# A graph network on one core: 56 first-stage tiles in fours for 48 in pairs, and a 224-word pause for a 320-word one behind each gather

## The chip, the cores and the metric

One core of a Trainium2 chip runs the whole program. The metric is the device time of one execution in microseconds (us). The kernel before took a median of 1958.26 us over 3 runs (1946.44 to 1959.8).

## What is computed

The input is 3125 nodes with 128 features each and 53125 edges, sorted by destination, each with one of 8 relations. Cut to its core:

```python
h = relu(layernorm(x))
for W, root, bias in ((W1, root1, b1), (W2, root2, b2), (W3, root3, b3)):      # three relational layers
    out = h @ root + bias
    for r in range(8):
        msg = where(edge_type == r, (h @ W[r])[src], 0)
        out += segment_sum(msg, dst) / max(count of edges of relation r into dst, 1)
    h = relu(out)
x = x + h
h = relu(layernorm(x))
x = x + batchnorm(relu((h + segment_sum(h[src], dst)) @ W1' + b1') @ W2' + b2') + h  # the last layer
```

## The kernel before, in words

The 53125 edges are cut into 416 tiles of 128 edges. For each relational layer L (0, 1, 2) TensorE first multiplies the node features with all eight relation matrices; the products (25 blocks of 128 nodes, 512 KB each) are stored by the SP queue as a table in device memory, `h_table`. Then, for every tile, GpSimd (POOL) issues one indirect DMA, a gather, that fetches the 128 rows that the tile's edges name into one of 24 slots of `rows` (line 1260; line 1281 for the first 11 tiles of layers 1 and 2, with the same cost). VectorE builds a small matrix `sel` per tile (`select`, line 966) that holds the weight of each edge in the column of its destination, and TensorE multiplies rows by `sel` into a sum in PSUM (`sum_tile`, line 564). Tiles are counted through all layers as G = 416 L + t.

Behind each gather GpSimd clears private words that nobody reads: `rest_a_while` (line 1244), a memset of `PAUSE` = 320 words in each of 128 partitions. In two ways gathers are held back: gather G, if even, waits until TensorE has finished the tiles up to G - 11 (`AHEAD_OF_PE` = 12, semaphore `s_mm`), and at a layer's start gathers wait for the table.

The first `FORE` = 48 tiles of layer 0 go another way, since the table of layer 0 is late. Their raw, normalised input rows are gathered while TensorE still makes the table (line 1249, each gather followed by two one-word memsets `beat`, the second waiting for the first, line 1238). `fore_tile` (line 582) then multiplies them by `fore_sel`, which keeps relations apart (384 columns, `fore_select`, line 915 on VectorE), into PSUM banks of 64 nodes. ScalarE copies each full bank (`key_whole`, line 744, two buffers), and `key_banks` (line 593) multiplies two banks at a time by the eight relation matrices into the sum of layer 0. VectorE's `match_tile` (line 944) counts edges for the weights of each tile; it needs a chunk of 16 tiles' keys, loaded by the SP queue (line 1107), and stays 8 tiles ahead of `select`.

How the two kinds of tile are mixed on TensorE is set by a list:

```python
head_order = [("fore", t) for t in range(FORE_RING)]                  # FORE_RING = 12
for t in range(FORE_RING, FORE, FORE_PACE):                           # FORE_PACE = 2
    head_order += [("tile", FORE + (t - FORE_RING) // FORE_PACE)] + [("fore", f) for f in range(t, t + FORE_PACE)]
HEAD = FORE + (FORE - FORE_RING) // FORE_PACE
```

VectorE follows it by batches: eight `select` (with eight matches), then the `fore_select` of the 8 * `FORE_PACE` first-stage tiles that stand beside them. `fore_select` f waits until TensorE has done first-stage tile f - 12, and TensorE waits at the first ordinary tile of each eight until all eight `select` are done.

Layer 1 also builds the dense adjacency that the last layer uses; layers 1 and 2 begin with `late_sums` (line 619, after tile 12). After layer 2 the last layer has no gathers and ends the program.

Of the kernel before, what the change touches and what calls it, by code (L numbers as in the profile page):

```python
# [2 lines left out]

# [13 lines left out]
P = 128  # L17
# [16 lines left out]
SLOTS = 24  # L34
BATCH = 8
FREE = 2
PAUSE = 320
AHEAD_OF_PE = 12
SELS = 32
CHUNK = 16  # L40
# [19 lines left out]
FILLS = 4  # L60
REGS = 16

FORE = 48
FORE_RING = 12
FORE_PACE = 2
FORE_SPAN = 48
FORE_LEAD = 18
KEY_BANK = 64
# [23 lines left out]
def gnn_kernel(nc, x, src_t, dst_t, type_t, limits, w_rel, root_w, bias_w,  # L92
# [17 lines left out]
    FORE_STEP = start_of[BATCH] - start_of[0]  # L110
    fore_start = [FORE_STEP * (t // BATCH) + STEP * (t % BATCH) - FORE_LEAD for t in range(FORE)]
    FORE_SLACK = max(P * t // DEG - FORE_LEAD - s for t, s in enumerate(fore_start))
# [60 lines left out]

    assert FORE % BATCH == 0

# [49 lines left out]
    with ExitStack() as ctx:  # L225
        def sb(name, shape, dt=F32):
            return ctx.enter_context(nc.sbuf_tensor(name, shape, dt))

        def sem(name):
            return ctx.enter_context(nc.semaphore(name))  # L230
# [32 lines left out]
        count = sb("count", [P, 2, BATCH])  # L263
        col_i = sb("col_i", [P, 1], I32)
        rest = sb("rest", [P, 4 * P])
        beat = sb("beat", [P, 1])
        slow = sb("slow", [P, 2, PAUSE])


# [141 lines left out]
        s_xn = sem("s_xn")  # L411
        s_xturn = sem("s_xturn")
        s_xT = sem("s_xT")
        s_beat = sem("s_beat")
        s_rested = sem("s_rested")
        s_row = [sem(f"s_row{n}") for n in range(SLOTS)]
        s_sel = sem("s_sel")
# [800 lines left out]
        def _(pool):  # L1218
# [10 lines left out]
            pool.wait_ge(s_src, 32)  # L1229
            pool.wait_ge(s_x0, 16 * GROUPS)  # L1230

            beats = itertools.count()

            def pause():
                made = next(beats)
                if made:
                    pool.wait_ge(s_beat, made)
                nc.gpsimd.memset(beat[:], 0.0).then_inc(s_beat, 1)

            def rest_a_while(G):  # L1240

                if G % 2 == 0 and G > FORE:
                    pool.wait_ge(s_rested, (G - FORE) // 2)
                done = nc.gpsimd.memset(slow[:, G % 2, :], 0.0)  # L1244
                if G % 2 == 1:
                    done.then_inc(s_rested, 1)

            for t in range(FORE):
                pool.indirect_dma_start(fore_rows[:, t, :], None, x0_table,  # L1249
                                        bass.IndirectOffsetOnAxis(ap=src_i[:, t:t + 1], axis=0)  # L1250
                                        ).then_inc(s_fore_row[t // BATCH], 16)
                pause()
                pause()
            pool.wait_ge(s_idx, 1)
            pool.wait_ge(s_flag, 1)
            fast = pool.value_load(flag[0:1, 0:1], min_val=0, max_val=1)
# [6 lines left out]
            with pool.If(fast != 0):  # L1263
                for L in range(GIN):
# [6 lines left out]
                    for t in range(0 if L else FORE, TILES):  # L1271
                        G = TILES * L + t
# [552 lines left out]
```

## Time and profile before

| | |
|---|---|
| median of 3 runs | 1958.26 us (1946.44 to 1959.8) |
| profiled execution: time, and span of its instructions | 1950.05 us, 1948.0 us |
| mean granted TensorE clock | 0.63 |
| busy: PE, DVE, ACT, POOL | 67%, 46%, 34%, 85% |

The profile comes from one execution. Engines are PE (TensorE; PEld its weight loads), DVE (VectorE), ACT (ScalarE) and POOL (GpSimd). A granted clock of 1.00 is 2.4 GHz and 0.50 is 1.2 GHz; between them is a mean over a stretch at both. The square brackets of a timeline row say how long the engine sat idle before the row and what ended it; "issue" means that it waited for nothing that the profile shows.

### The profile page before, as it was taken

What the parts mean: (1) busy time and instruction counts of PE and PEld (TensorE: products, weight loads), DVE (VectorE), ACT (ScalarE), POOL (GpSimd) and SP (SyncE); (2) the same over time, 40 slices, a digit from 0 to 9 for tenths busy, and PEclk for the clock granted to TensorE, in tenths of its full rate; (3) what the DMA queues carried; (4) which work ended last, traced back from release to release, by engine and by line L of the source; (5) the groups of instructions that cost most, each with busy time, mean ns of one, the idle gap of its engine ahead of it and who ended that gap; (6) DMA issues with size and microseconds to landing.
All of it is one profiled execution on the core that took longest, in us unless ns stands there. A gap on an engine that the chain in (4) does not pass through costs nothing.

```text
span 1948.0 us, 18786 instructions
## 1 busy us (share of the span) xinstructions
PE 1314.2 (67%) x4604; PEld 853.1 (44%) x4627; DVE 899.4 (46%) x3270; ACT 654.3 (34%) x1147; POOL 1663.3 (85%) x2550
## 2 busy tenths in 40 slices
PE   6798674747566786666676767676566565657677
PEld 2275343434344464343343434455444444444454
DVE  5485845444543266666566766651222212122213
ACT  5312200000000277777677776742001111102123
POOL 5768888888888888888888888888888888888882
PEclk9697755555555655657565756565567676757678
DMA  7552332323332311212121222231111111111111
GB/s 241 176 152 85 100 99 78 99 78 89 89 89 65 98 44 44 88 44 87 45 87 45 76 55 73 58 99 44 45 44 43 45 44 43 45 44 44 45 45 47
DMA packets 70011, 144.26 MB, mean 74 GB/s; under 512 B 23487, under 2 KB 37048, under 8 KB 69896
## 3 DMA queue, kind: packets, MB, share of 16 engines
q0 software_dynamic: 39840, 81.67, 16.6%
q1 hardware_dynamic: 29624, 60.67, 8.9%
q8 instruction: 41, 0.67, 0.2%
q10 hardware_dynamic: 432, 0.64, 0.1%
q14 instruction: 74, 0.61, 0.1%
HBM read 100.23 MB, written 42.67 MB: 73 GB/s over the span
## 4 chain that ended last, share of the span: by engine, by line
POOL 75%; issue 11%; PE 10%; DMA 3%; ACT 1%; DVE 1%; another core or an unknown queue 0%; SPq 0%; POOLq 0%; DVEq 0%
POOL rows L1260 53%; POOL slow L1244 22%; PE ps_h L533 3%; DMA rows<-h_table,idx 2%; PE ps_a L582 1%; PE ps_agg L564 1%; PE ps_agg L619 1%; PE ps_agg L593 1%; POOL rows L1281 1%; PE ps_h L671 0%; PE ps_a L671 0%; ACT early L735 0%; DMA x_rows<-in_x 0%; PE ps_agg L542 0%; DMA h_table<-scratch 0%
## 5 line engine op out<-in xcount | busy, mean ns | idle before, releaser
L1260 POOL DMA_INDIRECT rows<-h_table,idx x1175 | 1121.5, 954 | 215.7 <-issue 189.4
L564 PE MATMUL ps_agg<-sel,rows 128*128 128x64 f32 (+14 forms) x2764 | 755.0, 386 | 579.5 <-DMA rows<-h_table,idx 566.9
L564 PEld LDWEIGHTS ps_agg<-sel,rows 128*128 128x128 f32 x2764 | 627.9, 287 | 915.0 <-DMA rows<-h_table,idx 718.3
L966 DVE TENSOR_SCALAR sel<-iota,early,norm 128x64 f32<-128x64 f32 x1178 | 419.6, 429 | 496.7 <-PE ps_agg L564 493.9
L1244 POOL MEMSET slow<- 128x320 f32 x1200 | 462.7, 386 | 0.6
L1062 DVE TENSOR_TENSOR early<-ps_a,early 128x300 f32 x416 | 198.3, 477 | 218.6 <-PE ps_a L651 181.3
L848 ACT ACTIVATE scratch<-scratch,ones 128x300 bf16<-128x300 f32 x416 | 223.7, 538 | 116.1 <-PE ps_a L651 90.9
L533 PE MATMUL ps_h<-w_all,xT 128*128 128x512 f32 x300 | 228.5, 873 | 17.9 <-issue 17.2
L854 ACT ACTIVATE scratch<-iota,code_lo 128x300 f32<-128x300 f32 x416 | 226.5, 545 | 12.5
L944 DVE TENSOR_SCALAR_CACHE_REDUCE agg_s<-scratch,key_f 128x256 bf16<-128x256 int16 x416 | 196.5, 479 | 18.8 <-DMA scratch<-key_rows 14.0
L651 PE MATMUL ps_a<-scratch 128*128 128x300 bf16 x416 | 174.3, 420 | 2.9 <-DVE early L1062 1.2
L1051 DVE TENSOR_SCALAR scratch<-iota,code_lo 128x128 bf16<-128x128 f32 x416 | 153.9, 371 | 0.0
L755 ACT COPY stage<-ps_h 128x512 f32<-128x512 f32 x80 | 46.7, 585 | 242.9 <-PE ps_h L533 212.5
L760 ACT ACTIVATE xT<-ps_agg,vecs 128x512 f32<-128x512 f32 (+2 forms) x16 | 9.5, 591 | 294.8 <-PE ps_agg L564 294.5
L651 PEld LDWEIGHTS ps_a<-scratch 128*128 128x128 bf16 x416 | 97.0, 233 | 6.4 <-issue 6.1
L533 PEld LDWEIGHTS ps_h<-w_all,xT 128*128 128x128 f32 x300 | 68.6, 266 | 58.1 <-issue 51.2
L820 ACT CAST stage<-early 128x3072 bf16<-128x3072 uint8 x13 | 35.7, 2750 | 171.5 <-PE ps_a L671 143.4
L755 DVE COPY stage<-ps_h 128x512 f32<-128x512 f32 x50 | 34.2, 684 | 119.5 <-PE ps_h L533 118.9
L1249 POOL DMA_INDIRECT early<-x_table,early x48 | 45.7, 952 | 23.0 <-DMA x_table<-early 16.4
L820 ACT CAST w_all<-early 128x3072 bf16<-128x3072 uint8 x12 | 32.9, 2751 | 78.6 <-PE ps_a L671 76.8
L767 ACT ACTIVATE hid<-ps_agg,vecs 128x512 f32<-128x512 f32 (+3 forms) x10 | 5.3, 526 | 150.4 <-PE ps_agg L564 141.4
L671 PE MATMUL ps_a<-w_all,scratch 128*128 128x512 bf16 x104 | 40.3, 504 | 0.3
(159 smaller groups left out, 781.0 us busy)
## 6 DMA issues: line engine op xcount, KB each, us to landing
h_table<-stage SPq DMA_DIRECT2D x65, 512.0 KB
rows<-h_table,idx POOLq DMA_INDIRECT x1175
scratch<-key_rows SPq DMA_DIRECT2D x26, 544.0 KB
h_table<-scratch SPq DMA_DIRECT2D x10, 512.0 KB
x_rows<-in_x SPq DMA_DIRECT2D x6, 256.0 KB, 6.3
w_all<-in_W SPq DMA_DIRECT2D x3, 512.0 KB, 6.6
x_table<-early SPq DMA_DIRECT2D x6, 256.0 KB, 2.3
out<-early SPq DMA_DIRECT2D x6, 256.0 KB
```

Of the source, the lines that this page charges most:

```text
L533: nc.tensor.matmul(half_bank(L, b, half)[:], xT[:, block_of(b)], w_all[:, L, 4 * half:4 * half + 4, :].rearrange("p r o -> p (r o)"), star ...
L564: mm = nc.tensor.matmul(sums_of(L, k)[:, at:at + width], mine, sel[edges, G % SELS, in_window:in_window + width], start=False, stop=(t == ...
L651: nc.tensor.matmul(ps_a[a % A_BANKS][:, 0:HOT], low[:, a % HOTS, :], hot[:, a % HOTS, :], start=True, stop=True).then_inc(s_step, 1)
L755: copy(stage_of(H)[:, 512 * half:512 * half + 512], half_bank(L, b, half)[:]).then_inc((s_evA, s_evD)[half], 1)
L848: nc.scalar.activation(hot[:, a % HOTS, :], apart[:, a % 2, :], ACT.Relu, bias=ones[:, 0:1], scale=-1.0).then_inc(s_hot, 1)
L854: nc.scalar.activation(apart[:, a % 2, :], iota[:, EARLY:EARLY + HOT], ACT.Abs, bias=code[:, a:a + 1]).then_inc(s_apart, 1)
L944: done = nc.vector.tensor_scalar(match[:, t % BATCH, :], chunks[:, c % 2, at:at + 2 * P], key_f[:, t:t + 1], 0.0, ALU.is_equal, ALU.add, a ...
L966: done = nc.vector.tensor_scalar(mine, here, dst, weight, ALU.is_equal, ALU.mult)
L1051: nc.vector.tensor_scalar(low[:, a % HOTS, :], iota[:, EARLY:EARLY + P], lo_f[:, a:a + 1], None, ALU.is_equal).then_inc(s_low, 1)
L1062: nc.vector.tensor_tensor(mine, ps_a[a % A_BANKS][:, 0:HOT].rearrange("p (b d) -> p b d", d=REACH), mine, ALU.add).then_inc(s_add, 1)
L1244: done = nc.gpsimd.memset(slow[:, G % 2, :], 0.0)
L1260: pool.indirect_dma_start(rows[:, slot, :], None, table, bass.IndirectOffsetOnAxis(ap=column, axis=0)).then_inc(landed, 16)
```

## The change

`FORE` goes from 48 to 56 and `FORE_PACE` from 2 to 4: 56 tiles are made by the first-stage way, and behind the first twelve, one ordinary tile stands before each four of them. Layer 0 gathers 8 tiles fewer from the table, 11 ordinary tiles instead of 18 are mixed in (`HEAD` 67 for 66), and there are 7 banks of 64 nodes instead of 6. `PAUSE` goes from 320 to 224, and the first-stage gathers are followed by the same pause instead of the two `beat` memsets.

```diff
-PAUSE = 320
+PAUSE = 224
...
-FORE = 48
+FORE = 56
 FORE_RING = 12
-FORE_PACE = 2
+FORE_PACE = 4
...
-            beats = itertools.count()
-
-            def pause():
-                made = next(beats)
-                if made:
-                    pool.wait_ge(s_beat, made)
-                nc.gpsimd.memset(beat[:], 0.0).then_inc(s_beat, 1)
-
             def rest_a_while(G):
 
-                if G % 2 == 0 and G > FORE:
-                    pool.wait_ge(s_rested, (G - FORE) // 2)
+                if G % 2 == 0 and G:
+                    pool.wait_ge(s_rested, G // 2)
                 done = nc.gpsimd.memset(slow[:, G % 2, :], 0.0)
                 if G % 2 == 1:
                     done.then_inc(s_rested, 1)
...
-                pause()
-                pause()
+                rest_a_while(t)
```

VectorE, from the first twelve `fore_select` (128x384) to the first `select` (`sel`), before; 128x256 is a match, in eights with their reciprocal:

```order
L915 TENSOR_SCALAR early<-iota,rest,norm 128x384 x12
L944 TENSOR_SCALAR agg_s,count<-scratch,key_f 128x256 x8
L952 RECIPROCAL norm<-count 128x8
L944 TENSOR_SCALAR agg_s,count<-scratch,key_f 128x256 x8
L952 RECIPROCAL norm<-count 128x8
L944 TENSOR_SCALAR agg_s,count<-scratch,key_f 128x256 x8
L952 RECIPROCAL norm<-count 128x8
L966 TENSOR_SCALAR sel<-iota,early,norm 128x64
```

The same place of the change:

```order
L912 TENSOR_SCALAR early<-iota,rest,norm 128x384 x12
L941 TENSOR_SCALAR agg_s,count<-scratch,key_f 128x256 x8
L949 RECIPROCAL norm<-count 128x8
L941 TENSOR_SCALAR agg_s,count<-scratch,key_f 128x256 x8
L949 RECIPROCAL norm<-count 128x8
L941 TENSOR_SCALAR agg_s,count<-scratch,key_f 128x256 x8
L949 RECIPROCAL norm<-count 128x8
L941 TENSOR_SCALAR agg_s,count<-scratch,key_f 128x256 x8
L949 RECIPROCAL norm<-count 128x8
L963 TENSOR_SCALAR sel<-iota,early,norm 128x64
```

Eight more matches stand ahead of the first `select`, so 64 tiles are matched there instead of 56, and the match behind the first `select` is of tile 64, the first of the fifth chunk, instead of tile 56.

VectorE at the end of the first batch of eight `select`, before:

```order
L944 TENSOR_SCALAR agg_s,count<-scratch,key_f 128x256
L952 RECIPROCAL norm<-count 128x8
L915 TENSOR_SCALAR early<-iota,rest,norm 128x384 x16
L966 TENSOR_SCALAR sel<-iota,early,norm 128x64
L944 TENSOR_SCALAR agg_s,count<-scratch,key_f 128x256
```

And of the change:

```order
L941 TENSOR_SCALAR agg_s,count<-scratch,key_f 128x256
L949 RECIPROCAL norm<-count 128x8
L912 TENSOR_SCALAR early<-iota,rest,norm 128x384 x32
L963 TENSOR_SCALAR sel<-iota,early,norm 128x64
L941 TENSOR_SCALAR agg_s,count<-scratch,key_f 128x256
```

32 `fore_select` instead of 16 follow each batch.

TensorE at the end of the first-stage tiles, before (`ps_a` are their banks, `ps_agg` the sum of the layer; 128x128 x8 is `key_banks`):

```order
L564 MATMUL ps_agg0<-sel,rows 128x51
L564 MATMUL ps_agg1<-sel,rows 128x13
L582 MATMUL ps_a2<-early 128x384 x2
L593 MATMUL ps_agg0<-hid,w_all 128x128 x8
L564 MATMUL ps_agg0<-sel,rows 128x44
L564 MATMUL ps_agg1<-sel,rows 128x20
```

And of the change:

```order
L579 MATMUL ps_a2<-early 128x112
L579 MATMUL ps_a0<-early 128x272
L579 MATMUL ps_a2<-early 128x56
L579 MATMUL ps_a0<-early 128x328
L579 MATMUL ps_a0<-early 128x384 x2
L590 MATMUL ps_agg0<-hid,w_all 128x128 x8
L590 MATMUL ps_agg0<-hid,w_all 128x64 x8
L561 MATMUL ps_agg0<-sel,rows 128x37
L561 MATMUL ps_agg1<-sel,rows 128x27
```

The last pair of banks now has a seventh bank behind it, with a `key_banks` of its own, and the next ordinary tile (tile 67) comes after both.

## Rows read from the trace of the kernel before

**Rows 1.** POOL by line: count | busy us, mean ns of one | idle before, who ended it

```profile
L1260 POOL DMA_INDIRECT rows<-h_table,idx x1175 | 1121.5, 954 | 215.7 <-issue 189.4 <-DMA h_table<-scratch 17.7 <-PE ps_agg L564 8.6
L1244 POOL MEMSET slow<- 128x320 f32 x1200 | 462.7, 386 | 0.6
...
L1238 POOL MEMSET beat<- 128x1 f32 x96 | 11.5, 120 | 4.7 <-POOL beat L1238 1.9
...
L1814 POOL MEMSET const-float32-1.0<- 128x1 f32 x1 | 0.1, 98 | 0.0
```

**Rows 2.** The waits: engine line waited for: us in total, times, longest

```profile
PE ps_agg L564 <- DMA rows<-h_table,idx: 566.9, 748, 2.9
```

**Rows 3.** Windows: length, PE, PEld, DVE, ACT, POOL busy (count), PEclk, DMA share, GB/s

```profile
108.00:158.00 50.00, 47.35 (x244) 38.51 (x244) 48.55 (x174) 3.51 (x6) 41.39 (x60) 1.00 0.34 99
158.00:663.00 505.00, 322.81 (x944) 216.52 (x944) 238.07 (x1039) 41.50 (x61) 449.01 (x674) 0.55 0.30 88
702.00:1288.00 586.00, 402.84 (x1408) 243.48 (x1406) 383.70 (x1204) 427.59 (x826) 521.68 (x780) 0.59 0.23 65
1327.00:1911.00 584.00, 370.31 (x1433) 253.30 (x1450) 126.61 (x465) 94.71 (x89) 519.66 (x779) 0.66 0.18 44
```

**Rows 4.** POOL in order of time: start us, us, instruction [idle before, who ended it]

```profile
40.78 0.94 POOL L1249 DMA_INDIRECT early<-x_table,early  x1
...
42.14 0.94 POOL L1249 DMA_INDIRECT early<-x_table,early  x1
...
223.33 0.95 POOL L1260 DMA_INDIRECT rows<-h_table,idx  x1 [0.17 <-issue]
224.28 0.38 POOL L1244 MEMSET slow<- 128x320 f32 x1
224.83 0.95 POOL L1260 DMA_INDIRECT rows<-h_table,idx  x1 [0.16 <-issue]
```

**Rows 5.** POOL in order of time, where it stood still, a slow gather, the last gather

```profile
108.36 0.94 POOL L1260 DMA_INDIRECT rows<-h_table,idx  x1 [17.69 <-DMA h_table<-scratch]
...
158.35 0.95 POOL L1260 DMA_INDIRECT rows<-h_table,idx  x1 [3.84 <-PE ps_agg L564]
...
700.62 0.95 POOL L1260 DMA_INDIRECT rows<-h_table,idx  x1 [1.12 <-PE ps_agg L564]
...
1411.83 1.40 POOL L1260 DMA_INDIRECT rows<-h_table,idx  x1 [0.16 <-issue]
...
1910.89 0.95 POOL L1260 DMA_INDIRECT rows<-h_table,idx  x1 [0.17 <-issue]
```

**Rows 6.** DVE in order of time, head of layer 0

```profile
101.97 0.48 DVE L944 TENSOR_SCALAR_CACHE_REDUCE agg_s<-scratch,key_f 128x256 bf16<-128x256 int16 x1 [9.76 <-DMA scratch<-key_rows]
...
105.54 0.31 DVE L966 TENSOR_SCALAR sel<-iota,early,norm 128x64 f32<-128x64 f32 x1
...
110.76 8.62 DVE L915 TENSOR_SCALAR early<-iota,rest,norm 128x384 f32<-128x384 f32 x16
```

**Rows 7.** SP queue in order of time: loads of key chunks (L1107) and weights (L1172)

```profile
96.72 0.42 SPq L1107 DMA_DIRECT2D scratch<-key_rows  x1
...
103.59 1.49 SPq L1172 DMA_DIRECT2D w_all<-in_W  x2
105.12 47.91 SPq L1107 DMA_DIRECT2D scratch<-key_rows  x4
```

**Rows 8.** PE in order of time, head of layer 0

```profile
113.74 0.41 PE L564 MATMUL ps_agg<-sel,rows 128*128 128x64 f32 x2 [1.87 <-DMA rows<-h_table,idx]
...
146.48 1.52 PE L582 MATMUL ps_a<-early 128*128 128x192 f32 x8
...
153.29 3.98 PE L593 MATMUL ps_agg<-hid,w_all 128*128 128x128 f32 x16 [0.68 <-ACT hid L744]
```

**Rows 9.** Windows behind the head: the clock across a thin stretch (166 to 170 us)

```profile
166.00:170.00 4.00, 0.88 (x5) 0.49 (x3) 3.81 (x18) 0.58 (x1) 3.67 (x6) 1.00 0.82 257
170.00:175.00 5.00, 4.43 (x12) 2.57 (x13) 3.47 (x14) 0.00 (x0) 4.43 (x7) 0.60 0.32 105
```

More of the change, by code:

```diff
@@ L1 @@
-import itertools
 from contextlib import ExitStack
@@ L265, in gnn_kernel @@
         rest = sb("rest", [P, 4 * P])
-        beat = sb("beat", [P, 1])
         slow = sb("slow", [P, 2, PAUSE])
@@ L413, in gnn_kernel @@
         s_xT = sem("s_xT")
-        s_beat = sem("s_beat")
         s_rested = sem("s_rested")
```

## The prediction

> **What bounds the kernel now.** I read the lines of POOL first, then the waits, then the windows by stage, then POOL in order of time. POOL is 85% busy in the whole span, and two kinds of work make that up: 1175 gathers of 954 ns and 1200 pauses of 386 ns [rows 1]. What it does not spend on them is mostly a gap of 0.16 to 0.17 us between a pause and the next gather, which the view calls "issue": 189.4 us in total [rows 1]. In order of time an ordinary period is gather 0.95, pause 0.38, gap 0.17: starts at 223.33 and 224.83, 1.50 us apart [rows 4]. From 158 to 1911 us this runs almost without a break: POOL waits for TensorE only 8.6 us in the whole run, of which 3.84 at 158.35 and 1.12 at 700.62 [rows 1, 5]. Everyone else waits for the gathers: TensorE's tile matmuls stood 566.9 us in 748 waits for gathered rows [rows 2]. Its busy share is 64% (322.81 of 505 us) in layer 0, 69% in layer 1 and 63% in layer 2, at a mean granted clock of 0.55 to 0.66 [rows 3]. So the time from 158.35 to the last gather at 1910.89 is 1170 periods of GpSimd, and what remains is a head of 158 us and an end of 1948.0 - 1910.89 = 37.1 us.
>
> In the head it is different. From 108 to 158 us DVE is busy 48.55 and PE 47.35 of 50 us [rows 3], and POOL, though it starts at 108.36 when the table has landed, stands still in the end because it may run only 12 tiles ahead of TensorE [rows 5].
>
> **The pause: 96 words fewer.** No 224-word memset is in the trace. A memset of one word takes 98 ns alone and 120 as `beat`, one of 320 words 386 [rows 1]. The slope is (386 - 98) / 319 = 0.90 or (386 - 120) / 319 = 0.83 ns a word, so 96 words are 80 to 87 ns; I take 84. The bounds: nothing, if the period has a floor that the pause only fills; and 0.3 * 386 = 116 ns, if the whole duration scales with the words. 1170 periods by 84 ns are 98 us off (0 to 136). All of it lies on the path as long as TensorE keeps up: the period becomes 1.42 us, and the 69% share of layer 1 becomes 0.69 * 1.50 / 1.42 = 73%. That such a pace is possible for gathers is shown by the first stage, which ran at 42.14 - 40.78 = 1.36 us [rows 4].
>
> **The first-stage gathers.** 56 by about 1.42 us instead of 48 by 1.36 end some 14 us later, near 105 us, still before the table's landing at 108.36 [rows 5]. They are hidden; their 0.5 MB more beside the table's stores may push the landing by a microsecond, which I put into the head.
>
> **The head.** Here the change costs. The place to watch is tile 78's gather, which started at 158.35 [rows 5]: the periods behind it are the same tiles in both kernels. The 8 gathers that leave layer 0 buy nothing if this one starts no earlier. Its condition is TensorE past tile 67, and that tile stands behind all first-stage work.
> - DVE starts matching tiles 48 to 55 at 101.97, when its chunk has landed, and reaches the first `select` at 105.54 [rows 6], 3.4 us later. In the change eight more matches come first, so it is there near 109. Behind the first `select` it now needs tile 64, of a chunk whose load was issued at 105.12, behind two 512 KB weight loads at 103.59 [rows 7]. The chunk before it took 5.3 us, from its issue at 96.72 to DVE's use at 101.97 [rows 6, 7]. This one has more ahead of it: I take 113 to 114 us for its arrival (109 to 117). Then seven more pairs of `select` and match at 0.63 us: the eighth `select` ends near 118.5.
> - TensorE does its first ordinary tile then, at about 118.5 and not at 113.74 [rows 8]. That is 5 us lost, and an idle stretch of some 7 us.
> - From there, 44 first-stage tiles instead of 36. Two of them take 1.52 us [rows 8], so 8 more are 6.1 us. Seven ordinary tiles fewer at 0.2 give back 1.4.
> - At the end ScalarE must copy the seventh bank, into a buffer that the `key_banks` ahead of it is still reading. So TensorE waits about 1.2 us (before, it waited 0.68 for the sixth [rows 8]), and then does a `key_banks` of half the width: between a half and the whole of 3.98 us, I take 2.3.
> - Clock: after the thin stretch at 166 to 170 us TensorE's granted clock was 0.60, while it had been 1.00 in the head [rows 9, 3]. An idle stretch of 7 us in the head may do the same. I take 2 us for it (0 to 10).
>
> Sum: 5 + 6.1 - 1.4 + 0.5 + 2.3 + 2 + 1 (the landing) = 15.5. Tile 78's gather starts near 174 instead of 158.35: 15 us lost (5 to 27). DVE's 32 `fore_select` in a row do not add to it: two of them take 8.62 / 8 = 1.1 us [rows 6] and TensorE's two 1.5, so the ring of twelve stays full.
>
> The rule of the Trainium skill on the clock (TensorE: Matmul & The Clock Gate, Part 1) says that idleness takes the array to half its rate and sustained activity gives it back. By that rule the first-stage tiles behind the gap would start at half rate; the trace agrees in direction with 0.60 behind the thin stretch.
>
> **Starts of layers 1 and 2.** At 700.62 the gather waited 1.12 for TensorE, which had `late_sums` to do [rows 5]. That point follows from the tables and not from the pause, so the 26 gathers from the last of layer 0 gain nothing there: 26 * 84 ns = 2.2 us lost. At layer 2's start the same point was reached without a wait but close to it; I take 1.2.
>
> **Sum.** -98 + 15 + 3.4 = -79.6 us. Against the profiled execution: 1950.05 - 79.6 = 1870.5 (span 1868.4). The median of the runs lies 8 us higher, so the same sum gives 1878.7 there. I predict 1873.
>
> **Rivals.**
> - *TensorE takes over.* At 1.2 GHz its work per tile is near the new period wherever transforms or dense products are mixed in. For: granted clock 0.55 in layer 0 with 64% busy [rows 3]. Against: POOL waited 8.6 us in all. If a fifth of the 98 us is not given, 1893.
> - *A floor eats half.* The gather's own work could go on under the pause, so that shortening the pause moves the wait into the gather or the gap. For: the gap of 0.17 is unexplained. Against: 1.36 in the first stage. Half of 98 gives 1873 + 49 = 1922. The Trainium skill speaks for it (Perfetto Trace Analysis, DMA Instruction — SWDGE): the profile shows no start of such a DMA and ends it when the last descriptor is written, while the processor still has to finish the instruction. By that rule there is hidden work behind the 0.95 us; the row of 1.36 says that it is no floor at 1.42.
> - *The floor eats all of it.* Then the 98 us are missing: 1873 + 98 = 1971, within 1% of before.
> - *Slower: close gathers disturb each other.* A gather took 1.40 instead of 0.95 us at 1411.83 [rows 5]; few do now. If closer spacing made one in four do so, the mean grows by 0.25 * 0.45 = 0.11 us, 1170 of them 131 us: 1873 + 131 = 2004. It decides from a mean growth of 0.07 us (80 / 1170) on. For: the first stage ran at 1.36 us for 48 gathers only, not for 1170. Against: its gathers took 0.94 us, no more than those of the longer period [rows 4].
>
> **How the numbers follow.** The forecast has 0.70, TensorE as bound 0.07, half a floor 0.08, a whole one 0.04, slower 0.11. A measurement of this kernel can tell about 1% from no change. Faster by over 1% is 0.70 + 0.07 + 0.08 = 0.85, within 1% 0.04, slower 0.11. The pause at 80 to 90 ns and the head at 5 to 27 us give 1852 to 1893 for the forecast itself; the range goes up to half a floor, 1925.
>
> **What would show it.** Right: pauses of about 300 ns, gathers of 0.95, a period near 1.41 to 1.42, the eighth `select` near 118 us, tile 78's gather near 174 us, POOL waiting for TensorE some 25 us or more in the head alone, an end of 37 us behind the last gather. Wrong: gathers above 1 us in the mean, a gap that grew from 0.17, rows landing late with TensorE's waits unchanged, or POOL waiting for TensorE all through layers 0 and 1.

## The result and the profile after

The changed kernel takes 1935.01 us (median of four runs, 1931.12 to 1939.61) beside 1959.03 us for the kernel before: 0.9891 of it, with a 95% interval of 0.9843 to 0.9939. The direction of the prediction was right, its size wrong: 80 us were forecast, 24 came. The profiled execution took 1936.56 us, its span is 1934.5 us.

The costliest groups of the page of the changed kernel, as in [rows 1] and [rows 2] (busy us and mean ns of one, then the idle time before them and what ended most of it):

```profile
L1248 POOL DMA_INDIRECT rows<-h_table,idx x1167 | 1117.7, 958 | 282.6 <-issue 184.0
L561 PE MATMUL ps_agg<-sel,rows 128*128 128x64 f32 (+14 forms) x2748 | 674.4, 365 | 316.4 <-DMA rows<-h_table,idx 277.5
L1233 POOL MEMSET slow<- 128x224 f32 x1248 | 380.0, 305 | 0.9
L648 PE MATMUL ps_a<-scratch 128*128 128x300 bf16 x416 | 161.2, 388 | 245.3 <-issue 151.3
L1059 DVE TENSOR_TENSOR early<-ps_a,early 128x300 f32 x416 | 196.1, 471 | 247.6 <-remote 132.6
```

The pause took 305 ns where [rows 1] had 386: 81 ns less, as forecast. A gather takes 958 ns (954 before), and the gap is still 184.0 / 1167 = 0.16 us. So the gather has no floor of its own at this distance, and close gathers do not slow each other. But TensorE waited for rows only 277.5 us and not 566.9 [rows 2], and two groups that hardly waited before now do: the adjacency products of layer 1 on TensorE (L648, idle 245.3 us; 2.9 before) and VectorE's add behind them.

GpSimd in order of time answers to [rows 4, 5]. An ordinary period, then the table's landing, tile 78, tile 440 (layer 1), tile 448, tile 828 and tile 1246, the last gather:

```profile
start us, us, engine line op out<-in xcount [idle before <-releaser]
...
111.06 0.95 POOL L1248 DMA_INDIRECT rows<-h_table,idx  x1 [8.63 <-DMA h_table<-scratch]
...
175.96 0.95 POOL L1248 DMA_INDIRECT rows<-h_table,idx  x1 [12.48 <-PE ps_agg L561]
...
300.77 0.95 POOL L1248 DMA_INDIRECT rows<-h_table,idx  x1 [0.17 <-issue]
301.73 0.30 POOL L1233 MEMSET slow<- 128x224 f32 x1
302.19 0.95 POOL L1248 DMA_INDIRECT rows<-h_table,idx  x1 [0.17 <-issue]
...
706.47 0.95 POOL L1248 DMA_INDIRECT rows<-h_table,idx  x1 [8.88 <-PE ps_agg L561]
...
717.86 0.95 POOL L1248 DMA_INDIRECT rows<-h_table,idx  x1 [0.17 <-issue]
...
1280.16 0.95 POOL L1248 DMA_INDIRECT rows<-h_table,idx  x1 [1.06 <-remote]
...
1892.63 0.95 POOL L1248 DMA_INDIRECT rows<-h_table,idx  x1 [0.16 <-issue]
```

The ordinary period is 302.19 - 300.77 = 1.42 us, as forecast. The same tiles in both traces show where the time went (starts of the gathers; the sum, 13.5 us less, is the difference of the two profiled spans, while the medians lie 24 us apart):

| stretch, tiles | before | after | difference | forecast |
|---|---|---|---|---|
| up to tile 78 | 158.35 | 175.96 | +17.6 | +15.5 |
| 78 to 414, layer 0 | 503.40 | 484.74 | -18.7 | -28.2 |
| 414 to 448, start of layer 1 | 51.20 | 57.16 | +6.0 | -0.7 |
| 448 to 828, layer 1 | 571.23 | 562.30 | -8.9 | -31.9 |
| 828 to 864, start of layer 2 | 52.79 | 60.96 | +8.2 | -1.8 |
| 864 to 1246, layer 2 | 573.92 | 551.51 | -22.4 | -32.1 |
| behind the last gather | 37.1 | 41.9 | +4.8 | 0 |

(Forecast: 84 ns for each period, less the 2.2 and 1.2 us of the two starts.) The head came as forecast; the layers gave far less, and layer 1 least.

The head's own rows, VectorE first. Tile 48's match, the first `select`, the match that waits for the next chunk, the eighth `select`:

```profile
start us, us, engine line op out<-in xcount [idle before <-releaser]
103.90 0.48 DVE L941 TENSOR_SCALAR_CACHE_REDUCE agg_s<-scratch,key_f 128x256 bf16<-128x256 int16 x1 [15.72 <-DMA scratch<-key_rows]
110.85 0.32 DVE L963 TENSOR_SCALAR sel<-iota,early,norm 128x64 f32<-128x64 f32 x1
115.11 0.48 DVE L941 TENSOR_SCALAR_CACHE_REDUCE agg_s<-scratch,key_f 128x256 bf16<-128x256 int16 x1 [3.94 <-DMA scratch<-key_rows]
...
119.25 0.31 DVE L963 TENSOR_SCALAR sel<-iota,early,norm 128x64 f32<-128x64 f32 x1
```

And TensorE at both ends of the first-stage work:

```profile
start us, us, engine line op out<-in xcount [idle before <-releaser]
119.61 0.43 PE L561 MATMUL ps_agg<-sel,rows 128*128 128x64 f32 x2 [4.48 <-DVE sel L963]
120.80 2.93 PE L579 MATMUL ps_a<-early 128*128 128x384 f32 x4 [0.75 <-issue]
...
166.60 3.89 PE L590 MATMUL ps_agg<-hid,w_all 128*128 128x128 f32 x16
171.22 3.67 PE L590 MATMUL ps_agg<-hid,w_all 128*128 128x64 f32 x16 [0.73 <-ACT hid L741]
```

### The profile page after: what moved, and what is told of

The parts are those of the page before. It is cut to its first block, busy times and chain, and to the rows that moved or that the text cites. A ratio compares the mean times of both kernels' runs of the same rounds, so it can differ in the third digit from the quotient of the medians.

```text
span 1934.5 us, 18805 instructions
## 1 busy us (share of the span) xinstructions
PE 1232.1 (64%) x4633; PEld 867.5 (45%) x4656; DVE 857.4 (44%) x3270; ACT 644.0 (33%) x1148; POOL 1574.5 (81%) x2502
## 4 chain that ended last, share of the span: by engine, by line
POOL 37%; PE 21%; issue 19%; another core or an unknown queue 11%; ACT 6%; DVE 4%; DMA 2%; DVEq 0%; SPq 0%; ACTq 0%; POOLq 0%
POOL rows L1248 28%; POOL slow L1233 9%; PE ps_h L530 5%; PE ps_a L648 5%; PE ps_agg L561 5%; ACT scratch L845 4%; PE ps_a L579 2%; DVE early L1059 2%; PE ps_agg L616 1%; DMA rows<-h_table,idx 1%; ACT scratch L851 1%; PE ps_agg L590 1%; PE ps_agg L539 1%; DVE sel L963 1%
## 5 line engine op out<-in xcount | busy, mean ns | idle before, releaser
L1248 POOL DMA_INDIRECT rows<-h_table,idx x1167 | 1117.7, 958 | 282.6 <-issue 184.0
L561 PE MATMUL ps_agg<-sel,rows 128*128 128x64 f32 (+14 forms) x2748 | 674.4, 365 | 316.4 <-DMA rows<-h_table,idx 277.5
L963 DVE TENSOR_SCALAR sel<-iota,early,norm 128x64 f32<-128x64 f32 x1170 | 374.4, 363 | 516.7 <-PE ps_agg L561 349.5
L1233 POOL MEMSET slow<- 128x224 f32 x1248 | 380.0, 305 | 0.9
L648 PE MATMUL ps_a<-scratch 128*128 128x300 bf16 x416 | 161.2, 388 | 245.3 <-issue 151.3
L1059 DVE TENSOR_TENSOR early<-ps_a,early 128x300 f32 x416 | 196.1, 471 | 247.6 <-remote 132.6
L530 PE MATMUL ps_h<-w_all,xT 128*128 128x512 f32 x300 | 219.0, 839 | 54.9 <-issue 30.2
L941 DVE TENSOR_SCALAR_CACHE_REDUCE agg_s<-scratch,key_f 128x256 bf16<-128x256 int16 x416 | 192.6, 471 | 24.4 <-DMA scratch<-key_rows 19.7
L648 PEld LDWEIGHTS ps_a<-scratch 128*128 128x128 bf16 x416 | 54.3, 131 | 290.4 <-issue 280.0
L1048 DVE TENSOR_SCALAR scratch<-iota,code_lo 128x128 bf16<-128x128 f32 x416 | 133.9, 322 | 0.0
L1238 POOL DMA_INDIRECT early<-x_table,early x56 | 53.6, 957 | 25.3 <-DMA x_table<-early 16.3
L579 PE MATMUL ps_a<-early 128*128 128x384 f32 (+39 forms) x186 | 44.7, 389 | 0.9 <-issue 0.7
```

Source lines behind the costliest of these rows:

```text
L530: nc.tensor.matmul(half_bank(L, b, half)[:], xT[:, block_of(b)], w_all[:, L, 4 * half:4 * half + 4, :].rearrange("p r o -> p (r o)"), star ...
L561: mm = nc.tensor.matmul(sums_of(L, k)[:, at:at + width], mine, sel[edges, G % SELS, in_window:in_window + width], start=False, stop=(t == ...
L579: mm = nc.tensor.matmul(ps_a[j % A_BANKS][:, at:at + width], fore_rows[:, t, :], fore_sel[:, t % FORE_RING, in_window:in_window + width], ...
L648: nc.tensor.matmul(ps_a[a % A_BANKS][:, 0:HOT], low[:, a % HOTS, :], hot[:, a % HOTS, :], start=True, stop=True).then_inc(s_step, 1)
L941: done = nc.vector.tensor_scalar(match[:, t % BATCH, :], chunks[:, c % 2, at:at + 2 * P], key_f[:, t:t + 1], 0.0, ALU.is_equal, ALU.add, a ...
L963: done = nc.vector.tensor_scalar(mine, here, dst, weight, ALU.is_equal, ALU.mult)
```

## Where layer 1 went: the ring between TensorE and VectorE

In layer 1 every tile also brings an adjacency product (`pairs`, L648) into one of three PSUM banks, and VectorE's `add` (L1059) empties it. Product a waits for add a - 3. Paired one to one in the trace, 20 of the 416 products of the kernel before began within 0.25 us of that add's end, and 327 in the changed one. The add came 0.65 us (median) behind the start of its product before, and 3.1 us after. That is odd, because the same product takes no longer than before (388 ns in the mean, 420 before). ScalarE's copies of the table's halves show the same thing in two rows each. Changed kernel, layer 1: TensorE's product of a first half, then ScalarE's copy of it.

```profile
start us, us, engine line op out<-in xcount [idle before <-releaser]
1008.09 1.91 PE L530 MATMUL ps_h<-w_all,xT 128*128 128x512 f32 x2
...
1013.68 0.59 ACT L752 COPY stage<-ps_h 128x512 f32<-128x512 f32 x1 [2.36 <-remote]
```

The product's record ends at 1008.09 + 1.91 = 1010.00, ScalarE stood idle for 2.36 us and yet started only at 1013.68. The trace also holds the updates of the semaphores. I took, for each matmul that updates one, the time from its modelled end to the next update. In layer 1 it is over 0.5 us for 10% of them in the kernel before (median 0.01 us) and for 67% in the changed one (median 1.17). This way of counting has a flaw: where the record of an update is missing, the next one stands in for it and looks late. In layer 1 of the kernel before 554 of TensorE's 622 updates are recorded, in the changed one 507 of 609. Counted the other way, from each recorded update back to the last modelled end, none is over 0.5 us late in the kernel before and 64% are in the changed one (median 1.0 us, the latest 7.3 us). The recorded updates of VectorE, ScalarE and GpSimd stand within 0.04 us of an end in both. So TensorE's completions, and only they, reach the others late. This is what the experiments had to explain.

## The experiments

**First occasion: the parts of the change, and the size of the pause.** Four kernels on one chip, kernel before 1951.93 us.

```diff
# e1, e3, e4: kernel before, only this line (224, 272, 128)
-PAUSE = 320
+PAUSE = 224
# e2: changed kernel
-PAUSE = 224
+PAUSE = 320
```

e1. 

> The kernel before with 224 instead of 320 words in each memset of the pause, and nothing else: 48 first-stage tiles, two between two others, the one-word beats as they were. In the changed kernel the median period fell as forecast (1.50 to 1.42 us), but tile 78's gather came 17.6 us later and layers 1 and 2 gave only some 9 and 22 us in place of 30. Theory A (the shorter period itself makes TensorE's completions late, so that the ring of three banks that its adjacency products share with VectorE's add paces layer 1): the same loss without any change in the first stage, so only the 17.6 us of the head come back: 1935 - 18 = 1917 us (1908 to 1926), and VectorE's add waits for TensorE all through layer 1. Theory B (the loss comes with the first stage's change, through an alignment of the tiles): the whole pause is given, 1959 - 98 + 3 = 1864 us (1855 to 1875).

e2. 

> The changed kernel with the pause put back to 320 words: 56 first-stage tiles, four between two others, and the memset pause in the first stage remain. Theory A: tile 78's gather is some 16 us late and nothing else is lost, TensorE's completions come on time again: 1959 + 15 = 1974 us (1968 to 1980). Theory B: the loss of some 40 us in layers 1 and 2 is here too, on top of the head: 2010 us or more.

e3. 

> The kernel before with a pause of 272 words, half of the step. 48 words are 1170 periods by 42 ns = 49 us. Theory A with a loss that sets in between (TensorE's late completions begin below some period): 1959 - 49 + 2 = 1912 us, as fast as the pause of 224 words or faster. Theory A with a loss in proportion (40 of 98 us): 1959 - 29 = 1930 us. Theory B: 1912 us, and slower than the pause of 224 words by 49 us.

e4. 

> The kernel before with a pause of 128 words: a period near 1.34 us if nothing else holds it. Theory A: no faster than with 224 words, 1900 to 1930 us, with GpSimd waiting for TensorE's count through all of layer 1 and in much of layers 0 and 2. Theory B, and no floor: 1959 - 1170 x 0.16 = 1772 us. If close gathers also disturb each other, gathers above 1 us in the mean and over 1935 us.

Measured:

| | us | ratio (interval) | us a tile in layers 0, 1, 2 | late updates in layers 0, 1, 2 |
|---|---|---|---|---|
| before, 320 words | 1951.93 | | 1.497, 1.503, 1.502 | 0%, 0%, 0% |
| e2, 320 words | 1957.15 | 1.0029 (1.0014 to 1.0044) | 1.497, 1.503, 1.501 | 0%, 0%, 0% |
| e3, 272 words | 1926.11 | 0.9863 (0.9827 to 0.9899) | 1.458, 1.483, 1.463 | 1%, 65%, 6% |
| e1, 224 words | 1911.81 | 0.9821 (0.978 to 0.9861) | 1.443, 1.478, 1.445 | 47%, 60%, 57% |
| e4, 128 words | 1922.84 | 0.9866 (0.9807 to 0.9925) | 1.448, 1.482, 1.445 | 62%, 56%, 64% |
| changed kernel | 1935.01 | 0.9891 (0.9843 to 0.9939) | 1.442, 1.480, 1.444 | 37%, 64%, 61% |

(Layer paces from the starts of the gathers of tiles 90 and 414, 448 and 828, 864 and 1246; "late" is the share of TensorE's recorded updates over 0.5 us behind the last modelled end. The paces and shares of before and of the changed kernel are those of their own profiles, and the changed kernel's time is from an occasion of its own.) Theory A holds and B falls: the loss is there with the pause alone (e1), and absent where only the first stage is changed (e2). e3 lies between its two figures for Theory A, nearer to the loss in proportion (1930 us). The loss depends on the distance of the gathers: with 320 words completions are prompt, with 272 they are late almost only in layer 1, with 224 everywhere, and below that the time gets no better. 1.44 us a tile in layers 0 and 2 and 1.48 in layer 1 is what TensorE then gives, whatever the pause. e2 cost 5 us and not 15, and its rows say why. The last store of the table, and TensorE's first ordinary tile:

```profile
start us, us, engine line op out<-in xcount [idle before <-releaser]
...
70.42 2.05 SPq L1084 DMA_DIRECT2D h_table<-scratch  x2
```
```profile
start us, us, engine line op out<-in xcount [idle before <-releaser]
...
110.36 0.66 PE L561 MATMUL ps_agg<-sel,rows 128*128 128x64 f32 x2 [29.34 <-DMA rows<-h_table,idx]
```

The last stores of the table were issued at 70.42, in the kernel before at 101.49 and in the changed one at 104.96. In the kernel before the gathers of the first stage stand 1.36 us apart [rows 4], here 1.50. e2 differs from the changed kernel in nothing but the words of the pause, which gave 1.42 us there. Between 20 and 100 us, while the table is made, 17 of the 43 recorded updates of TensorE are over 0.5 us late in the kernel before and none of 46 in e2. So the first stage's close gathers had held up the table in the kernel before too.

**Second occasion: the leash, the products, the kind of pause.** Another chip, kernel before 1935.28 us.

```diff
# e5: e1 and
-AHEAD_OF_PE = 12
+AHEAD_OF_PE = 20
# e6: e1 without lows(), hots(), pairs() and add() in layer 1
# e7: kernel before with
-PAUSE = 320
+PAUSE = 128
                 if G % 2 == 1:
                     done.then_inc(s_rested, 1)
+                pause()
# e8: e1 with
-FORE = 48
+FORE = 40
+FORE_PAUSE = 320
...
-                done = nc.gpsimd.memset(slow[:, G % 2, :], 0.0)
+                done = nc.gpsimd.memset(slow[:, G % 2, 0:FORE_PAUSE if G < FORE else PAUSE], 0.0)
...
-                pause()
-                pause()
+                rest_a_while(t)
```

e5. 

> The kernel of e1 (before with a pause of 224 words) with GpSimd allowed 20 tiles ahead of TensorE in place of 12. In e1 TensorE lags about ten us behind the gathers all through layer 1 and GpSimd touches its limit of 12 tiles again and again. If the limit is what costs (TensorE is late now and then, but fast enough on average), the longer leash gives back most of it: 1912 - 20 = 1892 us or less. If TensorE's own pace is the bound while the gathers are this close (my theory), the leash is only used up: 1905 to 1915 us, the same as e1, with a lag that grows to some 20 tiles' time.

e6. 

> The kernel of e1 with the adjacency products left out of layer 1 (no lows, no hots, no pairs, no add, so that the output lacks their part). In e1 layer 1 ran at (1251.39 - 689.89) / 380 = 1.478 us a tile, layers 0 and 2 near 1.445. If layer 1's loss is the ring of three banks between TensorE and VectorE, lengthened by TensorE's late completions, layer 1 falls to the pace of the other layers, 1.42 to 1.445: 380 x 0.035 = 13 us or more less, 1912 - 13 = 1899 us (1888 to 1902). If the completions are late for a reason that has nothing to do with what TensorE is doing, they are late here too and layer 1 gains nothing beyond that. If instead the close gathers have nothing to do with it and TensorE was simply full, layer 1 runs at 1.42 without any wait: 1890 us.

e7. 

> The kernel before with a pause of 128 words followed by a memset of one word that waits for the one before it, so that the period is put back to some 1.46 to 1.50 us with less than half of the words. If what makes TensorE late is the distance between the gathers (my theory), its completions are on time again outside layer 1 and GpSimd hardly waits: 1959 - 1170 x (1.50 - period), 1915 to 1959 us, above e4's 1923 where the period comes out at 1.47 or more. If it is the shortness of the memset itself (how long GpSimd's other units rest), they stay late as in e4 and the time is 1960 us or more.

e8. 

> The kernel of e1 with a pause of 320 words behind the first-stage gathers in place of two beats, and 40 of them in place of 48. In the run with 320 words everywhere the first stage's period was 1.50 us and the table's last stores were issued at 70.4 us, and at 101.5 in the kernel before, whose first stage ran at 1.36 us. If the close gathers of the first stage are what made the table late, the first table gather starts at 23 + 40 x 1.50 = 83 us without a wait for the table, and tile 78's near 140 us in place of 150.8: 1912 - 11 = 1901 us (1894 to 1905). If the early table of that run had another cause, GpSimd waits for it until 100 to 108 us again, with 8 tiles more to gather behind it: 1912 + 12 = 1924 us.

Measured: e5 1830.21 us (0.946, 0.9443 to 0.9477), e6 1837.48 (0.9496, 0.9479 to 0.9514), e7 1788.24 (0.9245, 0.9229 to 0.9261), e8 1838.71 (0.951, 0.9491 to 0.9528). All four came over 50 us below the figures expected for them. Not one update in these four traces came over 0.5 us late, neither in the head nor in the layers. The layers ran at 1.416 to 1.422 us a tile with 224 words and at 1.375 in e7 (e4's first two table gathers stand 107.72 - 106.39 = 1.33 us apart: the one-word memset adds only some 40 ns to that, so the period did not return to 1.46 us). These runs tell nothing on the leash or the ring; they say that the late completions may not be a property of the kernels alone, which the third occasion tests.

**Third occasion: is it the edits or where they ran?** Kernel before 1948.83 us. No kernel is new.

e9. 

> The changed kernel once more, unaltered. The last four kernels ran on another chip than the first four: there the kernel before took 1935 us and not 1952 to 1959, TensorE's semaphore updates came 0.01 us behind the modelled end of their matmul everywhere (on the first chip up to several us late wherever the gathers were 1.42 us apart), and a pause of 224 words gave 100 us and not 40. Theory C (how late TensorE's completions come behind close gathers depends on the chip, not on the kernel): where the kernel before is near 1935 us here, the changed one takes 1935 - 80 = 1855 us (1845 to 1865) by the prediction's own sum; where it is near 1955, 1935 us again. If the difference of the last runs came from their edits (a longer leash, no products, another first stage), the changed kernel is at 0.99 of the kernel before on any chip.

e10. 

> The kernel of e1 once more, unaltered: 224 words and nothing else. Theory C: 1935 - 98 + 3 = 1840 us (1835 to 1846) where the kernel before is near 1935 us, and 1912 us where it is near 1955. The difference to the changed kernel on the same chip is what the first stage's change costs: 15 us by the prediction, 23 on the first chip. If the edits made the difference and not the chip: 0.982 of the kernel before on any chip.

e11. 

> The kernel of e5 once more: 224 words and 20 tiles ahead in place of 12. Its first run has no twin with 12 on the same chip. Theory C: within 12 us of the kernel with 12 tiles where completions are on time (what GpSimd waited for in the head, 8 to 10 us, goes). Where they are late: the same as with 12 tiles if TensorE's mean pace is the bound, 20 us less or more if the limit is.

e12. 

> The kernel of e4 once more: 128 words. On the first chip it was no faster than 224 words (1923 to 1912 us). Theory C: where completions are on time there is no floor at 1.42 us, the period is 1.33, and the time 1840 - 1170 x 0.08 + 10 = 1756 us (1745 to 1775). With a floor of the gather's own between 1.33 and 1.42: 1790 us or more. On a chip like the first: 1920 us again.

Measured: e9 1929.15 us (0.9904, 0.987 to 0.9938), e10 1916.74 (0.9827, 0.9797 to 0.9856), e11 1921.63 (0.987, 0.9833 to 0.9906), e12 1917.67 (0.9834, 0.9799 to 0.987). All as on the first occasion, late completions included. The kernel of e5 took 0.946 of the kernel before there and 0.987 here: the edit is not the cause. e11 against e10 answers the question on the leash: with 20 tiles ahead TensorE's median lag behind a gather's start grew by 12 us in layer 1, from some 9 (changed kernel, and e10 within 0.3 us of it) to 21 us, layer 1 ran at 1.476 us a tile and not at 1.478, and nothing was gained. What holds is TensorE's pace while its completions are late, and not the limit on GpSimd. e9 - e10 = 12.4 us is the price of the first stage's change here.

**Fourth occasion.** Another chip, kernel before 1933.38 us. The kernels of e9, e6, e8 and e7.

e13. 

> The changed kernel, unaltered, for a chip of the kind on which e5 to e8 ran. There (the kernel before near 1935 us, TensorE's updates on time) the prediction's own sum gives 1935 - 80 = 1855 us (1845 to 1865) for it. On a chip of the other kind (the kernel before near 1950) 1929 to 1935 us again. The same kernel with 20 tiles ahead took 0.946 of the kernel before on the one chip and 0.987 on the other, so the chip makes the difference and not the edit; this run says what it does to the change itself.

e14. 

> The kernel of e6, 224 words and layer 1 without its adjacency products (its output lacks their part). On the chip where completions are late, layer 1 ran at (1253.94 - 680.47) / 388 = 1.478 us a tile with the products (e10). If the ring of three banks turns the late completions into the loss of layer 1, it runs at 1.42 to 1.445 here and the time is 1917 - 13 = 1904 us or less; if TensorE's own tile work were enough to hold it at 1.478, 1917 us. On a chip where they are on time: 1837 us as in e6.

e15. 

> The kernel of e8: 40 first-stage tiles with a pause of 320 words behind each, 224 words in the layers. On a chip where completions are late behind close gathers: the table is finished before 80 us as in e2 (70.4 us for its last store), the first table gather starts at 83 us without a wait, tile 78's near 140 us in place of 152 to 159, and the time is 1917 - 12 = 1905 us (1895 to 1910). If the early table of e2 was chance, 1925 us. On a chip where they are on time: 1839 us as in e8.

e16. 

> The kernel of e7: 128 words and a memset of one word behind them, period 1.37 us. On a chip where completions are late behind close gathers it is on the plateau of the pauses of 224 and 128 words, 1912 to 1925 us; if the short memset were what makes them late, it is no different, and if the distance alone does, neither, since 1.37 us is below 1.42. On a chip where they are on time: 1788 us as in e7.

Measured: e13 1856.6 us (0.9599, 0.9583 to 0.9615), e14 1838.09 (0.9505, 0.9489 to 0.9521), e15 1837.71 (0.9502, 0.9486 to 0.9518), e16 1786.75 (0.9245, 0.9229 to 0.926). Completions are prompt again, and here the changed kernel takes 76.8 us less than the kernel before; 80 had been forecast. No profile of the kernel before was taken on such an occasion, so this difference cannot be split by stages as the first one was. Its page, the lines that answer to those of the changed kernel's first profile above:

```profile
L1248 POOL DMA_INDIRECT rows<-h_table,idx x1167 | 1115.0, 955 | 221.9 <-issue 186.4
L561 PE MATMUL ps_agg<-sel,rows 128*128 128x64 f32 (+14 forms) x2748 | 747.1, 387 | 526.1 <-DMA rows<-h_table,idx 515.3
L1233 POOL MEMSET slow<- 128x224 f32 x1248 | 380.2, 305 | 0.9
L1059 DVE TENSOR_TENSOR early<-ps_a,early 128x300 f32 x416 | 198.0, 476 | 203.8 <-PE ps_a L648 199.4
L648 PE MATMUL ps_a<-scratch 128*128 128x300 bf16 x416 | 175.7, 423 | 3.7 <-DVE early L1059 2.9
```

Same instructions, same durations on GpSimd, but TensorE waits for rows again (515.3 us) and its adjacency products wait 3.7 us and not 245.3. The same pair of rows as above, a first half and ScalarE's copy, now meets at once (953.98 + 1.02 = 955.00):

```profile
start us, us, engine line op out<-in xcount [idle before <-releaser]
953.98 1.02 PE L530 MATMUL ps_h<-w_all,xT 128*128 128x512 f32 x2
...
955.04 0.59 ACT L752 COPY stage<-ps_h 128x512 f32<-128x512 f32 x1 [0.92 <-PE ps_h L530]
```

GpSimd in this run, tiles 78, 448, 828 and 1246: (1229.85 - 688.89) / 380 = 1.424 us a tile in layer 1.

```profile
start us, us, engine line op out<-in xcount [idle before <-releaser]
161.16 0.95 POOL L1248 DMA_INDIRECT rows<-h_table,idx  x1 [12.48 <-PE ps_agg L561]
...
688.89 0.95 POOL L1248 DMA_INDIRECT rows<-h_table,idx  x1 [0.16 <-issue]
...
1229.85 0.95 POOL L1248 DMA_INDIRECT rows<-h_table,idx  x1 [0.17 <-issue]
...
1823.68 0.95 POOL L1248 DMA_INDIRECT rows<-h_table,idx  x1 [0.16 <-issue]
```

Its table's last stores went out at 69.75, with 1.42 us between the first stage's gathers. So where completions are prompt, close gathers do not delay the table either. In e14, whose first stage is that of the kernel before (1.36 us), the last stores went out at 72.08 and the first table gather started at 90.77, 17.6 us ahead of the 108.36 of [rows 5]. That is about what the kernel before takes less on these occasions (1933 to 1935 us beside the 1950 of its profile).

**Fifth occasion: the same chip as the fourth, some four minutes later.** Kernel before 1951.91 us.

```diff
# e17: e8 with
-PAUSE = 224
+PAUSE = 128
...
+                if G >= FORE:
+                    if beats:
+                        pool.wait_ge(s_beat, len(beats))
+                    nc.gpsimd.memset(beat[:], 0.0).then_inc(s_beat, 1)
+                    beats.append(G)
```

e17. 

> What the runs point to, together: 40 first-stage tiles in place of 48 with a pause of 320 words behind each, and in the layers 128 words with a memset of one word behind them (period 1.37 us); the limit of 12 tiles stays. On a chip where TensorE's completions are on time: 1787 us as in e16, within 5 us. On a chip where they are late behind close gathers the first stage's longer pause keeps them on time until 80 us, the table is there when the 40th gather is done, and the layers run at the plateau of the shorter pauses: 1917 - 12 = 1905 us (1895 to 1912). If the early table of e2 was chance: 1920 us or more.

e18. 

> The kernel of e6 and e14 for a chip of the first kind, 224 words and layer 1 without its adjacency products (its output lacks their part). If the ring of three banks turns TensorE's late completions into the loss of layer 1, a tile there takes 1.42 to 1.445 us in place of 1.478, and the time is 1917 - 13 = 1904 us or less. If the tile work alone holds it at 1.478: 1917 us. On a chip where completions are on time: 1838 us again.

Measured: e17 1906.28 us (0.9772, 0.9737 to 0.9807), e18 1898.74 (0.9721, 0.9679 to 0.9762). Completions are late again, on the chip where they had been prompt, so it is the occasion and not the chip: that part of Theory C falls. e18 shows what the products are worth. Layer 1 between tiles 448 and 828, e10 with its products and then e18 without:

```profile
start us, us, engine line op out<-in xcount [idle before <-releaser]
708.48 0.95 POOL L1260 DMA_INDIRECT rows<-h_table,idx  x1 [0.17 <-issue]
...
1270.06 0.95 POOL L1260 DMA_INDIRECT rows<-h_table,idx  x1 [0.16 <-issue]
```
```profile
start us, us, engine line op out<-in xcount [idle before <-releaser]
706.23 0.95 POOL L1253 DMA_INDIRECT rows<-h_table,idx  x1 [0.17 <-issue]
...
1250.50 0.95 POOL L1253 DMA_INDIRECT rows<-h_table,idx  x1 [0.16 <-issue]
```

That is 561.58 against 544.27 us, 1.478 against 1.432 a tile, and 18.0 us in the whole time (1916.74 to 1898.74, two occasions of the same kind). Without the products the late completions remain (38% of the recorded updates over 0.5 us) and layer 1 runs like the other two, so its extra loss comes from the products. That it comes through the ring of three banks rests on the pairing above (327 of 416): e18 takes away not only the ring but also the work for it on TensorE, VectorE and ScalarE, and no run gave the products more banks. Where completions are prompt, the products cost 6 ns a tile (1.422 us in e5, 1.416 in e6). e17 shows the head's part: with 320 words in the first stage the table is out by 69.96 and the first table gather starts when the 40th gather is done, 25 us earlier than in the kernel before.

```profile
start us, us, engine line op out<-in xcount [idle before <-releaser]
...
69.96 2.05 SPq L1088 DMA_DIRECT2D h_table<-scratch  x2
```
```profile
start us, us, engine line op out<-in xcount [idle before <-releaser]
83.13 0.95 POOL L1259 DMA_INDIRECT rows<-h_table,idx  x1 [0.16 <-issue]
```

## Why the prediction was right in direction and wrong in size

- **The pause, 81 to 84 ns in each of 1170 periods: right as a duration, wrong as a gain.** The period is 1.42 us in every run with 224 words. The sentence that failed is "All of it lies on the path as long as TensorE keeps up". TensorE does not keep up on the occasions on which its completions are late. In the three layers' even stretches (1086 periods) the pause gave 18.0 + 8.9 + 22.4 = 49 us of 91, and the rival "TensorE takes over", which I gave 0.07 and a fifth of the 98 us, is what happened, with nearly a half, though not for the reason I gave: I put it down to work at 1.2 GHz, and in e13, where TensorE kept up, its mean granted clock was 0.63 as well (0.64 in the changed kernel's first profile). On the other kind of occasion the whole step stood: layers at 1.420 to 1.424 us, and 76.8 us in total. That the total comes so near to 80 is in part luck, since the head's term rests on a table that lands at 108.36, and there its last stores go out some 30 us earlier (see below).
- **"That such a pace is possible for gathers is shown by the first stage."** It was, for gathers. I looked only at the engine that I was speeding up. At that pace, where completions are late, TensorE and the stores needed 30 us more for the table (101.49 against 70.42 us in e2), and GpSimd's 17.69 us before the first table gather [rows 5] were the sign of it, which I read as something given.
- **Head, +15 (5 to 27): +17.6 measured, by other steps in part.** The eighth `select` began at 119.25 (forecast: ends near 118.5), the next chunk's match at 115.11 (113 to 114), TensorE idled 4.48 us and started its next tiles at half pace (2.93 us for two), the end of the first-stage work brought 0.73 us of wait and 3.67 us for the narrow `key_banks` (forecast 1.2 and 2.3: half the width did not halve it, with a granted clock of 0.56 from 170 to 180 us). In other pairs the first stage's change cost 23 us (changed kernel against e1, two occasions), 12.4 (e9 against e10), 5 (e2 against before) and some 18 us (e13 against e14, which also lacks the products). Part of the spread is the start of the first table gather, which moved by +10.3, -2.1, -0.6 and +12.2 us in these four pairs. The step "They are hidden", on the eight first-stage gathers more, failed on the prompt occasion: the table was out at 69.75, GpSimd reached the table's first gather at 102.97 where e14 has 90.77, and tile 78's at 161.16 where e14 has 140.16.
- **Starts of layers 1 and 2: mis-sized.** With their 2.2 and 1.2 us lost the table above expects -2.5 us for both stretches together; +14.2 was measured. GpSimd waited 8.88 us at 706.47, 1.12 in [rows 5]. From tile 828 to 864 it took 51.2 us in e13, where 51.0 had been forecast, and 61.0 here.
- **End of 37.1 us: 41.9 measured,** 38.3 in e13 (1862.0 - 1823.68).
- **Rivals on the gathers' floor and on gathers that disturb each other: both wrong.** Gathers took 0.952 to 0.958 us in the mean of every run, and 1.375 us a tile held for a whole run in e7. The Trainium skill (Perfetto Trace Analysis, DMA Instruction — SWDGE) says that the processor goes on after the end that the profile draws; no run here shows that rest, and none of the periods down to 1.375 us was held by it.
- **"Wrong if POOL waited for TensorE all through layers 0 and 1"**: it did so in layer 1, in many waits of about a microsecond. This sign was named, but with too little chance.
- What stays open: why TensorE's completions come late on one kind of occasion. The traces show when (gathers some 1.46 us apart or closer, and first in layer 1, which has the adjacency products), not through what. One rival is untested. On the late occasions records of updates are missing too, the more the closer the gathers: 21,305 were recorded for the kernel before, 13,813 in e3, 9,701 in e1 and 8,445 in e4, and none of TensorE's is missing in e5 and e13. Every execution listed here has a span and a clock from its own record, so whether the recording itself holds TensorE back on these occasions, or only suffers from the same thing, is not known.

## What to carry to other kernels

A wait between two gathers may be there for another engine's sake: before shortening it, look in the profile of before for a stretch that already runs at the shorter distance, and read there how the other engines do, not only the gathers. Where two engines hand buffers round a short ring (three banks here), its waits stay invisible while a third one sets the pace, and late signals cost most there. Measure a kernel that lives on such a balance on several occasions, with the old one beside it each time: the same change was worth 1% and 4%, and the kernel before itself told which it would be (1949 to 1959 us, or 1933 to 1935).

With late completions nothing was gained below 224 words (0.9821 in e1 and 0.9827 in e10, beside 0.9866 and 0.9834 with 128); e17, with 128 words and one more, and a longer pause in the first stage, took 0.9772. With prompt ones 128 words and a one-word memset gave 0.9245 (e7, e16). The pause of 128 words alone was not run there, nor the kernel of e7 with late completions.

## What was not expected of the hardware

- TensorE's semaphore updates came up to several microseconds behind the modelled end of their matmul (7.3 us at most in layer 1 of the changed kernel), while the gathers on GpSimd and their landing (2.2 us from start to last packet in both kinds) were unchanged. Share of the recorded updates over 0.5 us late in layer 1: none in e5, e13 and the kernel before, 65% in e3, 64% in the changed kernel.
- The Trainium skill (Perfetto Trace Analysis, Tensor Engine Instruction) says that the start of a matmul is recorded when it begins to fetch its data, that its end is computed from its size, and that the semaphore is updated when PSUM has acknowledged the last bytes. The prompt runs agree (0.01 us between the computed end and the update); in the late ones the time lies between the recorded start and that acknowledgement, where no row of a trace looks.
- The trace itself is thinner there: 9,395 semaphore updates were recorded for the changed kernel, 26,930 for the same kernel in e13, and the page has no landing time for its gathers where e13's gives 2.5 us.
- The kind of occasion changed on one chip within minutes, and all kernels of an occasion shared it.
